# Tiles of a mixture of experts: rows fetched through an inverse list instead of scattered, and tile 0 fixed to expert 0

## The reference

```python
xn = rms_w * (x * jax.lax.rsqrt(var + EPS))
gate = xn @ wg_W + wg_b + (genre_embed @ gg_W + gg_b)
gate_w = jax.nn.softmax(gate, axis=-1)
topk_w, topk_i = jax.lax.top_k(gate_w, TOP_K)
...
h1 = relu(x @ W1[e] + b1[e]); h2 = relu(h1 @ W2[e] + b2[e]); out_e = h2 @ W3[e] + b3[e]
y = sum over the two chosen e of weight_e * out_e
```

## Time and profile before

| | us |
|---|---|
| median of 3 runs | 1168.87 (1166.0 to 1169.07) |
| the profiled execution, its own time | 1178.05 |
| its span in the profile | 1176.3 |
| PE busy | 935.0 (79%) |
| DVE busy | 682.7 (58%) |
| ACT busy | 559.6 (48%) |
| POOL busy | 169.2 (14%) |
| DMA, mean rate | 150 GB/s |

### The profile page before, as it was taken

The page is one execution under the profiler, slowest core; times in us unless marked ns, Lnnn a source line. Parts: engine busy times, 40 slices in busy tenths (PEclk is TensorE's granted clock), DMA queues, the critical chain, the costliest instruction groups (busy, mean ns, idle before and its releaser), DMA issues. The chain is left out here.

```text
span 1176.3 us, 20791 instructions
## 1 busy us (share of the span) xinstructions
PE 935.0 (79%) x7292; PEld 798.8 (68%) x7292; DVE 682.7 (58%) x1146; ACT 559.6 (48%) x1094; POOL 169.2 (14%) x191
## 2 busy tenths in 40 slices
PE   4007999999994688886599998699997975867897
PEld 3007999999994466666477776699997863432476
DVE  3206777776772588893587786544442774211397
ACT  4005667675762466652667775533333432322322
POOL 0370111111011432202222222000000000000011
PEclk9558999999998799997899999799998986977799
DMA  8836999998880152213000000000006702998011
GB/s 283 327 109 233 327 334 332 310 346 326 318 307 19 54 162 31 49 19 90 1 1 1 0 0 1 1 1 1 1 1 237 318 36 108 377 425 378 27 65 53
DMA packets 84977, 176.68 MB, mean 150 GB/s; under 512 B 43176, under 2 KB 60584, under 8 KB 74536
## 3 DMA queue, kind: packets, MB, share of 16 engines
q1 hardware_dynamic: 74496, 134.79, 32.3%
q0 software_dynamic: 8224, 38.54, 9.0%
q10 hardware_dynamic: 2184, 2.38, 0.6%
HBM read 151.05 MB, written 22.54 MB: 148 GB/s over the span
## 5 line engine op out<-in xcount | busy, mean ns | idle before, releaser
L526 DVE TENSOR_TENSOR moe_wl<-moe_raw,moe_wh 128x1024 fp32r<-128x1024 f32 x92 | 110.9, 1220 | 47.3 <-issue 32.5
L81 PE MATMUL moe_pH<-moe_hh,moe_wh 128*128 128x256 f32 x368 | 102.3, 278 | 1.2 <-DVE moe_hl L535 1.2
L83 PE MATMUL moe_pH<-moe_hl,moe_wh 128*128 128x256 f32 x368 | 102.1, 277 | 0.0
L82 PE MATMUL moe_pH<-moe_hh,moe_wl 128*128 128x256 f32 x368 | 102.0, 277 | 0.0
L471 ACT ACTIVATE moe_wh<-moe_raw 128x1024 fp32r<-128x1024 f32 x46 | 48.5, 1056 | 94.2 <-DMA moe_raw<-in_w 94.0
L535 DVE TENSOR_TENSOR moe_hl<-moe_ht,moe_hh 128x512 fp32r<-128x512 f32 x92 | 63.4, 690 | 37.4 <-ACT moe_hh L495 37.1
L486 ACT ACTIVATE moe_ht<-moe_pH,moe_b 128x256 f32<-128x256 f32 x184 | 75.9, 463 | 16.0 <-PE moe_pH L83 15.6
L2122 POOL TENSOR_TENSOR tok_xb<-k_x,k_rows 128x512 f32<-128x512 f32 x8 | 10.2, 1272 | 430.7 <-POOLq L68 369.2
L81 PEld LDWEIGHTS moe_pH<-moe_hh,moe_wh 128*128 128x128 f32 x368 | 69.0, 188 | 1.4 <-DVE moe_hl L535 1.4
L82 PEld LDWEIGHTS moe_pH<-moe_hh,moe_wl 128*128 128x128 f32 x368 | 69.1, 188 | 0.0
L83 PEld LDWEIGHTS moe_pH<-moe_hl,moe_wh 128*128 128x128 f32 x368 | 69.1, 188 | 0.0
(11 more groups left out here) (324 smaller groups left out, 3057.6 us busy)
## 6 DMA issues: line engine op xcount, KB each, us to landing
moe_raw<-in_w SPq DMA_DIRECT2D x46, 512.0 KB, 5.3
moe_wh<-in_w POOLq DMA_DIRECT2D x23, 1024.0 KB, 8.7
moe_raw<-in_w SPq DMA_DIRECT2D x23, 1024.0 KB, 7.8
ring<-in_w_slot SPq DMA_DIRECT2D x11, 2048.0 KB, 19.9
ring<-in_w_slot SPq DMA_DIRECT2D x11, 1024.0 KB, 19.0
k_w_ff<-in_w_slot SPq DMA_DIRECT2D x4, 2048.0 KB
moe_xr<-rows_of_experts SPq DMA_DIRECT2D x23, 256.0 KB, 4.3
results_of_experts<-moe_ysb POOLq DMA_DIRECT2D x23, 256.0 KB, 4.1
```

The source lines that it names most:

```text
L81: nc.tensor.matmul(out, ah, bh, start=start, stop=False)
L82: nc.tensor.matmul(out, al, bh, start=False, stop=False)
L83: return nc.tensor.matmul(out, ah, bl, start=False, stop=stop)
L526: v.tensor_tensor(wl[a][l][:, n], raw_w[a][l][:, n], f32(wh[a][l][:, n]), ALU.subtract).then_inc(wl_ok[l], 1)
```

## The change

The zero fill, the array `xs` and the scatter are gone. Instead route computes the inverse list `g.row_of`: for each of the NQ = 46 half tiles (128 places each), which row of x stands at each place. It does so with one-hot products. For each of the 32 columns n of tokens (16 columns, two choices), `onplace[:, n, :]` is the one-hot of the token's place within its half tile (128 wide) and `row_half[:, n, :]` holds the token's row number in the column of its half tile (46 wide); their products, summed over n in PSUM, are the list. Places with no token get row 0. Each tile fetches its rows straight from x with two indirect loads of 128 rows from the POOL queue.

Tile 0 now always belongs to expert 0 (each expert gets at least one tile), so its weights are loaded and split in route, in buffers (`expert_weights`) that outlive it; the three low parts are made by POOL. x comes in four transfers. All eight transposed bodies are copied out by DVE. Squares are written over weight buffers of tile 1.

```diff
 def route(nc, g, dr):
+    w = expert_weights(nc, g, g.moe_scope)      # raw, hi, lo buffers and their semaphores
...
 @block.sync
-            sp.dma_start(g.x[:, :, :], dr.x_tm).then_inc(x_in, 16)
-            sp.wait_ge(zero_set, 1)
+            for q in range(4):
+                sp.dma_start(g.x[:, 4 * q:4 * q + 4, :], dr.x_tm[:, 4 * q:4 * q + 4, :]).then_inc(x_in[q], 16)
             sp.wait_ge(const_in, 16 * 4)
             sp.wait_ge(small_in, 16 * 7)
-            for j in range(0, NT * SLOT // P, 8):
-                sp.dma_start(xs[j:j + n]..., zero[:, 0:n * D]...).then_inc(zero_out, 16)
+            for l in range(3):
+                sp.dma_start(w.raw[0][l][:, :], dr.w[l][0]).then_inc(w.raw_in[0][l], 16)
...
 @block.gpsimd
-            nc.gpsimd.memset(zero[:, :], 0.0).then_inc(zero_set, 1)
+            pool.wait_ge(small_in, 16 * 7)
+            pool.dma_start(w.hi[0][1][:, :], dr.w[1][0]).then_inc(w.w2h_in[0], 16)
+            pool.wait_ge(w.raw_in[0][1], 16)
+            pool.wait_ge(w.w2h_in[0], 16)
+            nc.gpsimd.tensor_tensor(w.lo[0][1], w.raw[0][1], f32(w.hi[0][1]), ALU.subtract)      # 2048 wide
+            pool.wait_ge(in_half_ok, 1)
+            nc.gpsimd.tensor_tensor(row_half, in_half, rowid, ALU.mult).then_inc(row_half_ok, 1)  # 1472 wide
+            for l in (0, 2):
+                pool.wait_ge(w.hi_ok[l], 1)
+                nc.gpsimd.tensor_tensor(w.lo[0][l], w.raw[0][l], f32(w.hi[0][l]), ALU.subtract)   # 1024 wide
...
 @block.scalar
-                if t % 4 == 3: wait xT_ps; copy pT to xT
...
+            for l in (0, 2):
+                act.wait_ge(w.raw_in[0][l], 16)
+                nc.scalar.activation(w.hi[0][l][:, :], w.raw[0][l][:, :], ACT.Copy).then_inc(w.hi_ok[l], 1)
...
 @block.tensor
+            nc.tensor.matmul(pN, g.tri[:, P:2 * P], g.tri[:, 0:P], start=True, stop=True)         # 0..127 along a row
+            nc.tensor.matmul(pM, g.tri[:, 0:P], g.tri[:, P:P + 1], start=True, stop=True).then_inc(count_ps, 1)
...
+            pe.wait_ge(row_half_ok, 1)
+            for n in range(2 * TT):
+                if n % 8 == 0:
+                    pe.wait_ge(on_place, n // 8 + 1)
+                last = nc.tensor.matmul(pI, onplace[:, n, :], row_half[:, n, :], start=n == 0, stop=n == 2 * TT - 1)
+            last.then_inc(row_ps, 1)
...
 @block.vector
+            step(v.tensor_scalar(ntl[:, :], ntl[:, :], 1.0, None, ALU.max))
...
             for c, oh in enumerate((oh1, oh2)):
-                product with slotf, reduce, cast to g.slot[c]
+                step(v.tensor_tensor(tmp, oh, rank, ALU.mult))
+                step(v.tensor_reduce(rank_c[:, c, :], tmp, AX_X, ALU.add))
+                step(v.tensor_tensor(tmp, oh, bc(nin[1 - b], 1, TT), ALU.mult))
+                step(v.tensor_reduce(base_c[:, c, :], tmp, AX_X, ALU.add))
+            step(v.tensor_tensor(over, bc(rank_f, 2, 15), bc(grid[:, P:P + 15], 1, 2 * TT), ALU.is_ge))   # 480 wide
+            step(v.tensor_reduce(part[:, :], over[:, :, :], AX_X, ALU.add))
+            v.scalar_tensor_tensor(place, part, -float(P), rank_f, ALU.mult, ALU.add).then_inc(place_ok, 1)
+            step(v.scalar_tensor_tensor(half, base_f, float(SLOT // P), part, ALU.mult, ALU.add))
+            v.tensor_tensor(in_half, bc(half, 2, NQ), bc(grid[:, 0:NQ], 1, 2 * TT), ALU.is_equal).then_inc(in_half_ok, 1)
+            dve.wait_ge(place_ok, 1)
+            for i in range(0, 2 * TT, 8):                                                          # 4 times 1024 wide
+                v.tensor_tensor(onplace[:, i:i + 8, :], bc(place, 2, P), bc(grid[:, 0:P], 1, 8), ALU.is_equal).then_inc(on_place, 1)
...
+            dve.wait_ge(row_ps, 1)
+            v.tensor_copy(g.row_of[:, :], pI).then_inc(row_ok, 1)
...
 def experts(nc, g, dr):        # SP: rows(j) is gone from its queue; POOL:
-            cast(0)
+            def rows(j):
+                if j >= 2:
+                    pool.wait_ge(xT_ps, j - 1)
+                for s in range(2):
+                    nc.gpsimd.indirect_dma_start(
+                        out=xr[j % 2][:, s, :], out_offset=None, in_=x_rows,
+                        in_offset=bass.IndirectOffsetOnAxis(ap=g.row_of[:, 2 * j + s:2 * j + s + 1], axis=0)).then_inc(x_in[j % 2], 16)
+
+            rows(0)
             cast(1)
-            32 indirect scatters of g.x to dr.xs, by g.slot
+            rows(1)
             for j in range(2, NT):
+                rows(j)
                 cast(j)
                 store(j - 2)
```

More of the change, by code:

```diff
@@ L103, in route @@
         xT = sb("xT", [P, KD, T])
-        sq = sb("sq", [P, TT, D])
+        sq = [w.raw[1][0][:, t * D:(t + 1) * D] for t in range(4)] + [w.raw[1][1][:, t * D:(t + 1) * D] for t in range(8)] + [w.raw[1][2][:, t * D:(t + 1) * D] for t in range(4)]
         ss = sb("ss", [P, TT])
@@ L115, in route @@
         cum = [sb(f"cum{i}", [P, TT, E1]) for i in range(2)]
-        slotf = sb("slotf", [P, TT, E1])
+        rank = sb("rank", [P, TT, E1])
+        rank_c = sb("rank_c", [P, 2, TT])
+        base_c = sb("base_c", [P, 2, TT])
+        over = sb("over", [P, 2 * TT, 15])
+        part = sb("part", [P, 2 * TT])
+        half = sb("half", [P, 2 * TT])
+        place = sb("place", [P, 2 * TT])
+        slotf = sb("slotf", [P, 2 * TT])
+        grid = sb("grid", [P, P + 15])
+        first_row = sb("first_row", [P, 1])
+        rowid = sb("rowid", [P, TT])
+        in_half, row_half = (xT[:, k, 0:2 * TT * NQ].rearrange("p (n q) -> p n q", q=NQ) for k in range(KD))
+        onplace = g.x1[:, :, :].rearrange("p t c -> p (t c)").rearrange("p (n q) -> p n q", q=P)
         cmp1 = sb("cmp1", [P, E1, E1])
@@ L296, in _ @@
             step(v.tensor_tensor(nin[1 - b][:, :], nin[b][:, :], ntl[:, :], ALU.subtract))
[L297 to L300, removed]
+            step(v.tensor_tensor(rank[:, :, :], cum[a][:, :, :], pS[:, :, :], ALU.subtract))
@@ L301, in _ @@
+            step(v.tensor_tensor(rank[:, :, :], rank[:, :, :], pR[:, :, :], ALU.add))
             for c, oh in enumerate((oh1, oh2)):
[L302 to L305, removed]
+                step(v.tensor_tensor(tmp[:, :, :], oh[:, :, :], rank[:, :, :], ALU.mult))
+                step(v.tensor_reduce(rank_c[:, c, :], tmp[:, :, :], AX_X, ALU.add))
+                step(v.tensor_tensor(tmp[:, :, :], oh[:, :, :], bc(nin[1 - b][:, :], 1, TT), ALU.mult))
+                step(v.tensor_reduce(base_c[:, c, :], tmp[:, :, :], AX_X, ALU.add))
@@ new lines, in _ @@
+            rank_f = rank_c[:, :, :].rearrange("p c t -> p (c t)")
+            base_f = base_c[:, :, :].rearrange("p c t -> p (c t)")
+            step(v.tensor_tensor(over[:, :, :], bc(rank_f, 2, 15), bc(grid[:, P:P + 15], 1, 2 * TT), ALU.is_ge))
+            step(v.tensor_reduce(part[:, :], over[:, :, :], AX_X, ALU.add))
+            v.scalar_tensor_tensor(place[:, :], part[:, :], -float(P), rank_f, ALU.mult, ALU.add).then_inc(place_ok, 1)
+            step(v.scalar_tensor_tensor(half[:, :], base_f, float(SLOT // P), part[:, :], ALU.mult, ALU.add))
@@ new lines, in _ @@
+            v.tensor_tensor(in_half[:, :, :], bc(half[:, :], 2, NQ), bc(grid[:, 0:NQ], 1, 2 * TT), ALU.is_equal).then_inc(in_half_ok, 1)
+            dve.wait_ge(place_ok, 1)
+            for i in range(0, 2 * TT, 8):
+                v.tensor_tensor(onplace[:, i:i + 8, :], bc(place[:, i:i + 8], 2, P), bc(grid[:, 0:P], 1, 8), ALU.is_equal).then_inc(on_place, 1)
+            step(v.scalar_tensor_tensor(slotf[:, :], half[:, :], float(P), place[:, :], ALU.mult, ALU.add))
+            for c in range(2):
+                v.tensor_copy(g.slot[c][:, :], slotf[:, c * TT:(c + 1) * TT]).then_inc(slots, 1)
@@ L311, in experts @@
 def experts(nc, g, dr):
-    with ExitStack() as ctx:
+    with g.moe_scope, ExitStack() as ctx:
         sb, ps, sem = scope(nc, ctx, "moe")
[L314 to L317, removed]
+        w = g.moe_weights
+        raw_w, wh, wl = w.raw, w.hi, w.lo
+        raw_in, w2h_in, wh_ok, wl_ok = w.raw_in, w.w2h_in, w.hi_ok, w.lo_ok
```

104 lines of the change are left out of this document (54 added, 50 removed).

## The result

The change makes the kernel slower: 1240.43 us in the median (1234.8 to 1243.44) against 1168.74 before, a ratio of 1.061 (95% interval 1.057 to 1.065). The prediction was 1147, with a range of 1136 to 1163. It had the sign wrong and missed by 93 us. The profiled execution after has a span of 1238.7 us, 62.4 longer than before.

A forecast was written before the change was run, and what follows sets the result against it. The scatter's end was taken to set the experts' start, then PE's own pace to bind. An earlier start of -28.7, late rows +6 and drains +1 gave -21.7 us, from 1168.87 to 1147, range 1136 to 1163.

The forecast's parts named there:

- Step 1: Route's chain up to the list: `in_half` ready at about 43.4 us, the list copied at 57 us.
- The alternation of DVE and POOL: In route after `in_half`: the two engines take turns rather than run in parallel, 4.9 + 7.9 less 0.7, ending at 55.5 us.
- the price of the list's products: At the end of route: the last eight products, taken at 0.15 us each.
- Step 2: From the list at 57 us to the first expert product at 66 us, a start 28.7 us earlier.
- Step 3: Row loads behind the store in the tiles: rows land 0.3 us late on 21 tiles, +6 us.
- the landing: In each tile, second indirect load to turn: 3.3 us from issue, plus 0.4 for the raw weights issued then.
- The share for competition: Part of each tile's landing: 0.4 us for raw weights SP issues at the same moment, bounds 0 and 1.0.
- The hold of POOL by DVE: In the tiles: an indirect load issued beside a DVE low part takes 1.72 instead of 0.96 us, +0.76.
- Step 4: POOL's drains at block ends: +1 us after the experts; route 0.1, at worst 2.7.
- The rival "slower": Row loads in the tiles, everything at its end: 1.6 us late, 34 us over 21 tiles, 1175 us; chance 0.05.
- Its point of decision: Lateness of each tile's rows from which the rival "slower" decides: 1.3 us a tile (27.7 over 21).

The follow-up runs named there:

- run 2: The changed kernel with SP's raw weights of each tile held until that tile's rows have landed (tile 1's until tile 0's); 1174.06 us, ratio 1.000.
- run 4: The changed kernel with the computed list overwritten by 128 different rows for each half tile; 1225.54 us, ratio 1.042.
- Run 10: The kernel of run 8 with 150 idle transposes in place of 90; 1141.53 us, ratio 0.980.
- run 8: The changed kernel with rows issued before the store, 90 idle transposes before the list's products, copies shared with ScalarE, tile 1's weights held for tile 0's rows; 1147.0 us.
- run 3: The changed kernel with each indirect load replaced by a plain POOL load of 128 fixed rows at the same place; 1153.85 us, ratio 0.983.
- run 5: The kernel of run 3 with eight small POOL fills ahead of the plain row loads from tile 3 on; 1233.49 us, ratio 1.059.

## Why the prediction was wrong, by its steps

**Step 1, route's own chain: late by 6.4 us.** `in_half` was ready at 45.8 us, against 43.4 predicted. In the experiments it was ready at 43.8 to 44.3 us in eight profiled executions and at 46.0 and 46.3 in runs 2 and 4, whose edits don't touch that part, so some 2 us of this differ from one execution to the next. The alternation of DVE and POOL held nearly to the number, ending at 57.1 (predicted 55.5):

```profile
45.72 11.41 DVE L353 TENSOR_TENSOR k_x<-route_place,route_grid 128x1024 f32<-128x1024 f32 x4
...
45.88 3.57 POOL L183 TENSOR_TENSOR route_xT<-route_xT,route_rowid 128x1472 f32<-128x1472 f32 x1 [20.09 <-DVE route_xT L350]
49.42 6.63 POOL L187 TENSOR_TENSOR moew_wl<-moew_raw,moew_wh 128x1024 fp32r<-128x1024 f32 x2
```

Wrong was the price of the list's products, 0.15 us each. They took 13.89 us for 32, or 0.43 each, since the clock was 0.50 in that stretch. They ran without a gap from 49.51 to 63.4 and set the end themselves. The evidence was in the earlier trace rows: the stage had a clock of 0.50 before as well. Run 10 shows the clock as the cause: at 1.00 the products took 0.22 us each, 50 records in 5.5 us. Even there 0.15 would have been too low.

**Step 2, list to first product: late by 3.2 us more.** From the list's copy at 63.44 to the first product at 75.59 were 12.15 us; I had 8.9.

```profile
63.44 0.21 DVE L358 CAST moew_row_of<-route_pC 128x46 uint32<-128x46 f32 x1 [5.92 <-PE route_pC L257]
...
65.51 1.03 POOL L448 DMA_INDIRECT moe_xr<-in_x_tm,moew_row_of  x1 [9.46 <-POOLq L69]
66.84 0.95 POOL L448 DMA_INDIRECT moe_xr<-in_x_tm,moew_row_of  x1 [0.30 <-issue]
...
72.97 1.11 PE L472 MATMUL moe_pX<-k_ident,moe_xr 128*128 128x128 f32 x4 [9.57 <-DMA moe_xr<-in_x_tm,moew_row_of]
...
75.59 0.55 PE L82 MATMUL moe_pH<-moe_xh,moew_wh 128*128 128x256 f32 x1 [1.50 <-DVE moe_xl L589]
```

From the copy to the first load are 2.1 us, where the barrier was priced at 1.2. The second load took 6.1 us to the turn, where I had 3.3 and 0.5. With SP's weights of tile 1 held it took 3.7 (run 8). The start gained 19.1 us, not 28.7.

**Step 3, each tile's rows: the step that failed.** The forecast was +6 us; it was 87.0. The mechanism stands in the prediction, the load behind the store in the loop of PE, result, store and rows, and so does the rival of 1.6 us a tile, but no case reached 4.3, by which the 20 periods from tile 2 on grew (87.0 over 20). The mis-sized term is the landing, 3.3 + 0.4 us against 7.60 (7.4 in the mean). The 3.3 came from gathers that had the DMA engines nearly to themselves (the attention's start); the 4.3 us in the earlier trace rows was from loads that stood ahead of the weights in SP's own queue. The share for competition was bounded by 1.0, the distance from 3.3 to that 4.3, and so by a row of the old order: in the changed one 2 MB of weights are issued between the two loads of the rows, 1.5 us ahead of the second. Run 2 shows that they are worth some 3 us; between runs 3 and 5, where only the place moves, it is 1.4 in the medians. What I had not counted at all is the second round: after PE's wait the granted clock is 0.50 for 3.2 us, and `out_layer`, in the same loop, becomes 1 us longer. In all, the lower clock is 22.5 of the 87.0 us.

The hold of POOL by DVE was right. The indirect load beside L585 took 1.78 us, and the one behind it, with DVE free, 0.98, against 1.72 and 0.96 in the earlier trace rows; 20 of the 46 loads look like that. SP's issuing isn't the reason, though it often falls into the same time: in run 2 the load of 209.38 us took 1.81 beside L589, with SP's weights issued 6.8 us later. The Trainium skill ("SBUF — State Buffer", section "Who interferes with whom") has it, marked as inferred, that a `tensor_tensor` doesn't stall GpSimd's descriptor writing. The traces don't agree for an indirect load; the plain store beside the same operation took 0.74 us as ever. The same section has a second rule, that a VectorE instruction with two SBUF inputs contends with a GpSimd instruction that reads SBUF. An indirect load has its list in SBUF and a plain one has none, so this rule would fit both rows; no run here tests it.

**Step 4, block ends: right.** POOL's drain at the end of the experts:

```profile
L382 POOLq DRAIN  x1: 7496/7496/7496, 441.3 to 441.3; - x1
```

7.5 us against 7.4 predicted and 6.43 in the earlier trace rows. I gave route's drain 0.1 us; nothing in the trace waits for it.

The misses add up. The start is 9.6 us late (19.1 gained of 28.7), the experts 81.0 (87.0 for 6), and from the last turn to the end are 826.8 us, where 833.3 would be before's 832.3 and the drain's 1: 9.6 + 81.0 - 6.5 = 84.1, the distance from the predicted span of 1154.6 to 1238.7. The rival "slower" (0.05) had the right place and the wrong size. Its point of decision, 1.3 us a tile, was near enough to deserve more than 5 in 100, since its bounds rested on a share for competition that no row of this order had shown.

What stays open: how much of the 3 us is bandwidth and how much is the order in which the engines serve the queues. Nothing here separates the two.

## What to carry to other kernels

When a load is moved, draw the loop that it then stands in, from the wait that releases it to the work that waits for it, and add up the loop's length with the landing time under the traffic that is in flight there, not with one from a quiet stretch. A loop that is a little shorter than the period is no cover: 2.5 us of delay in it cost 85 us over 20 tiles (runs 3 and 5). The cure was free, to issue the load ahead of the instruction that waits on the same loop. And price small products that come after a silent stretch at the lower clock.

## What the runs showed of the hardware

- An indirect load of GpSimd that meets a running VectorE `tensor_tensor` of 1024 elements takes 1.78 us instead of 0.98. Plain loads (0.54 us, run 5) and stores (0.74) keep their time.
- From the second of two indirect loads (256 KB of rows), issued 1.5 us behind 2 MB of weights of another queue, to the work that waits for them are 7.6 us, and 4.6 when the weights wait.
- The list that a gather reads counts: the ratio to the kernel before is 1.061 with the padded places on row 0 and 1.042 with distinct rows at a fixed distance. Which of the two differences does it isn't shown.
- TensorE's clock stayed at 0.50 through 13.9 us in which the small products kept it busy, after 15 us of rest; with transposes up to the first product it was at 1.00 from there until 55 us, and at 0.50 from 56 us on, still without a gap. After a wait of 3.65 us for rows it was 0.50 for 3.2 us.
